# Cross-attention: the context's low part and the key norms' inverse root from VectorE to GpSimd, the denominators' first refining step kept in PSUM

## The reference

```
q = rmsnorm((x @ Wq) by head) * gq          k = rmsnorm((ctx @ Wk) by head) * gk      v = (ctx @ Wv) by head
rmsnorm(u) = u * rsqrt(mean(u * u) + 1e-5)
attn = softmax(q k^T / sqrt(128))            out = (attn v, all heads side by side) @ Wo
x = layernorm(x + self_attention(x));  x = layernorm(x + cross_attention(x, ctx));  x = layernorm(x + mlp(x))
```

## Time and profile before

| what | value |
|---|---|
| time, median of 3 runs | 1498.09 us (1496.63 to 1501.16) |
| the profiled execution's own time | 1501.96 us |
| its span, first to last instruction | 1500.1 us |
| mean granted TensorE clock | 0.987 of full speed |
| busy: TensorE | 1381.0 us, 92% |
| busy: VectorE | 1408.0 us, 94% |
| busy: ScalarE | 913.0 us, 61% |
| busy: GpSimd | 976.8 us, 65% |

### The profile page before, as it was taken

How to read it: one execution, slowest core, us unless ns; L and a number is a source line. 1 busy time by engine, 2 the same in 40 slices (tenths; PEclk the granted TensorE clock), 3 DMA queues, 4 the chain that set the end, 5 groups by cost and what they waited for, 6 DMA issues and landing times. The chain is left out here.

```text
span 1500.1 us, 23822 instructions
## 1 busy us (share of the span) xinstructions
PE 1381.0 (92%) x6430; PEld 1009.6 (67%) x6430; DVE 1408.0 (94%) x2023; ACT 913.0 (61%) x2744; POOL 976.8 (65%) x770
## 2 busy tenths in 40 slices
PE   7799899999999999999999999999999999988888
PEld 4678677666666666666666666666666666655678
DVE  5889799999999999999999999999999999999785
ACT  2645576666666666666666666666666666643443
POOL 4600005788777777887778777878787778876340
PEclk9899999999999999999999999999999999999999
DMA  6040010010101010101010101010101000010200
GB/s 224 30 150 1 23 42 21 1 41 1 42 1 42 1 42 0 41 1 41 1 41 1 39 3 34 8 32 10 32 11 31 11 15 6 20 59 1 86 1 25
DMA packets 17927, 45.56 MB, mean 30 GB/s; under 512 B 1600, under 2 KB 11968, under 8 KB 17040
## 3 DMA queue, kind: packets, MB, share of 16 engines
q1 hardware_dynamic: 17088, 44.24, 9.0%
q10 hardware_dynamic: 720, 0.10, 0.0%
HBM read 40.41 MB, written 3.93 MB: 30 GB/s over the span
## 5 line engine op out<-in xcount | busy, mean ns | idle before, releaser
L941 POOL TENSOR_TENSOR xa_scores<-xa_scores,xa_gmax 125x448 f32<-125x448 f32 x352 | 469.6, 1338 | 187.2 <-ACT xa_gmax L987 170.7
L1134 PE MATMUL xa_k_ps<-wk_parts,xa_ctxT_hi 128*125 128x512 f32 x768 | 428.6, 558 | 6.2 <-DVE wk_parts L1127 4.7
L888 POOL TENSOR_TENSOR xa_den<-probs,xa_den 125x448 f32<-125x448 f32 x311 | 370.4, 1191 | 86.4 <-ACT probs L1001 74.6
L980 ACT ACTIVATE xa_k_ps<-xa_k_ps 125x128 f32<-125x128 f32 x720 | 190.1, 264 | 324.6 <-DVE xa_ss L1060 220.7
L1071 DVE TENSOR_TENSOR xa_cmax<-xa_scores,xa_cmax 125x448 f32<-125x448 f32 x320 | 359.1, 1122 | 0.7
L1201 PE MATMUL xa_o_ps<-probs,xa_ctx_nat 125*128 125x448 f32 x768 | 352.7, 540 | 0.0
L1060 DVE TENSOR_REDUCE xa_ss<-xa_sq 125x6 f32<-125x768 f32 x360 | 337.2, 937 | 0.0
L1135 PE MATMUL xa_k_ps<-wk_parts,xa_ctxT_hi 128*125 128x512 f32 x768 | 303.8, 396 | 0.0
L1136 PE MATMUL xa_k_ps<-wk_parts,xa_ctxT_lo 128*125 128x512 f32 x768 | 303.8, 396 | 0.0
L982 ACT ACTIVATE xa_sq<-xa_k_ps 125x768 f32<-125x768 f32 x360 | 287.8, 799 | 0.0
L1001 ACT ACTIVATE probs<-xa_scores 125x448 f32<-125x448 f32 x384 | 219.3, 572 | 42.4 <-DVE xa_scores L1097 40.1
(11 more groups left out here) (170 smaller groups left out, 1754.4 us busy)
## 6 DMA issues: line engine op xcount, KB each, us to landing
ctxT_in<-in_ctxT SPq DMA_DIRECT2D x16, 750.0 KB, 9.1
xa_ctx_nat<-in_ctx SPq DMA_DIRECT2D x16, 750.0 KB
qo<-in_xq_w SPq DMA_DIRECT2D x1, 2048.0 KB, 11.1
qo<-in_xo_w SPq DMA_DIRECT2D x1, 2048.0 KB, 19.0
vo_scratch<-qo SPq DMA_DIRECT2D x2, 1024.0 KB, 4.2
vo<-vo_scratch SPq DMA_DIRECT2D x1, 2048.0 KB, 8.1
xq_wkT<-in_xk_wT SPq DMA_DIRECT2D x4, 256.0 KB, 4.2
probs<-in_xk_w SPq DMA_DIRECT2D x1, 1024.0 KB, 8.6
```

Of the source, the lines that this page charges most:

```text
L888: eng.tensor_tensor(den[:, hy, :], probs[0:KP, y % NPR, :], den[:, hy, :], ALU.add).then_inc(den_done, 1)
L941: pool.tensor_tensor(score_slot(y), score_slot(y), gmax[:, (y // KT) % 2, :], ALU.subtract).then_inc(shift_done, 1)
L980: act.activation(own, own, ACT.Square, accum_out=ss[:, j // 2, head:head + 1])
L1134: pe.matmul(out, l_hi, r_hi, start=True, stop=False)
```

## The change

Three things move. (1) `split_low`, the low part of the context, goes from VectorE to GpSimd; there it stands at the *start* of every fourth step, ahead of the subtraction, where on VectorE it stood at the end. (2) The Newton step on the key norms' inverse root goes to GpSimd as `refine_rk`, ahead of the subtraction of steps 2 and 14. GpSimd gets it in four operations on two tensors, for which a column of the constant 1.5 / sqrt(128) (`c15`) is broadcast, and the factors are folded into others: VectorE's mean is halved and scaled by `HALF`, which ScalarE's ln takes out again. (3) The closing's first result is written back to its bank of PSUM instead of to `cmax`, so the bank comes free (`s_taken`) after the second instruction instead of after the first.

```diff
--- before.py
+++ after.py
@@ -717,6 +717,7 @@
 EARLY = 3
 WH = 6
 QC = 4
+HALF = 0.5 * XD ** -0.5
 QW = UW // QC
 MAX_TURN, MAX_SPREAD = 1, 2
 
@@ -832,6 +833,7 @@
         nt = lg
         rk = sb("xa_rk", [KP, 2, KT, XH])
         ones = sb("xa_ones", [KP, 1])
+        c15 = sb("xa_c15", [KP, 1])
         ident = sb("xa_ident", [P, P], F32R)
         ident_in = probs[:, NPR - 1, 0:P]
         qmax = sb("xa_qmax", [QW, QC], F32R)
@@ -919,19 +921,47 @@
         @block.gpsimd
         def _(pool):
             pool.memset(ones[:, :], 1.0).then_inc(ones_set, 1)
-            pool.wait_ge(ones_set, 1)
+            pool.memset(c15[:, :], 1.5 * XD ** -0.5).then_inc(ones_set, 1)
+            pool.wait_ge(ones_set, 2)
 
             def q_low(ph, h):
                 pool.wait_ge(qhi_ready, ph.at(2, h + 1))
                 pool.tensor_tensor(q_lo[:, h, :, :], qo[:, UH * h:UH * h + UH, ph.tokens()],
                                    q_hi[:, h, :, :].bitcast(F32), ALU.subtract).then_inc(qlo_ready, 1)
 
+            def split_low(ph, c):
+                i = ph.parity()
+                pool.wait_ge(hi_ready, ph.at(KT // 2, c + 1))
+                pool.tensor_tensor(ctxT_lo[:, i, 2 * c:2 * c + 2, :], ctxT_in[:, i, 2 * c:2 * c + 2, :],
+                                   ctxT_hi[:, i, 2 * c:2 * c + 2, :].bitcast(F32), ALU.subtract).then_inc(lo_ready, 1)
+
+            def refine_rk(ph, ahead, g):
+
+                n = 3 if ahead else 2
+                rk_g = rk[:, ph.shift(ahead).parity(), g, :]
+                pool.wait_ge(table_ready, ph.at(2, n))
+                pool.tensor_tensor(nt[:, :, :], rk_g, rk_g, ALU.mult).then_inc(newton, 1)
+                pool.wait_ge(newton, ph.at(6, 3 * (n - 1) + 1))
+                pool.tensor_tensor(nt[:, :, :], nt[:, :, :], ss[:, g, :], ALU.mult).then_inc(newton, 1)
+                pool.wait_ge(newton, ph.at(6, 3 * (n - 1) + 2))
+                pool.tensor_tensor(nt[:, :, :], c15[:, :].unsqueeze(2).broadcast_to([KP, KT // 2, XH]), nt[:, :, :],
+                                   ALU.subtract).then_inc(newton, 1)
+                pool.wait_ge(newton, ph.at(6, 3 * (n - 1) + 3))
+                pool.tensor_tensor(rk_g, rk_g, nt[:, :, :], ALU.mult).then_inc(rk_ready, 1)
+
+            split_low(Phase(0), 0)
+
             def body(ph):
                 if ph.b == -1:
                     q_low(Phase(0), 0)
-                    return
                 for j in range(STEPS):
                     h, t = divmod(j, KT)
+                    if split_at(ph, j):
+                        ahead, c = split_at(ph, j)
+                        split_low(ph.shift(ahead), c)
+                    for step, ahead, g in ((13, 1, slice(0, 6)), (1, 0, slice(6, 12))):
+                        if j == step + 1 and ph.shift(ahead).within(0, 15):
+                            refine_rk(ph, ahead, g)
                     y = lagged(ph, j, SHIFT_LAG)
                     if y is not None and not vector_shifts(ph, y):
                         if y % KT == 0:
@@ -1004,7 +1034,7 @@
                         if j == step and ph.shift(ahead).within(0, 15):
                             n = ph.at(2, 3 if ahead else 2)
                             act.wait_ge(mean_ready, n)
-                            act.activation(lg[:, :, :], ss[:, g, :], ACT.Ln).then_inc(ln_ready, 1)
+                            act.activation(lg[:, :, :], ss[:, g, :], ACT.Ln, scale=1.0 / HALF).then_inc(ln_ready, 1)
                             act.wait_ge(ln_ready, n)
                             act.activation(rk[:, ph.shift(ahead).parity(), g, :], lg[:, :, :], ACT.Exp, scale=-0.5
                                            ).then_inc(table_ready, 1)
@@ -1028,12 +1058,6 @@
 
         @block.vector
         def _(dve):
-            def split_low(ph, c):
-                i = ph.parity()
-                dve.wait_ge(hi_ready, ph.at(KT // 2, c + 1))
-                dve.tensor_tensor(ctxT_lo[:, i, 2 * c:2 * c + 2, :], ctxT_in[:, i, 2 * c:2 * c + 2, :],
-                                  ctxT_hi[:, i, 2 * c:2 * c + 2, :].bitcast(F32), ALU.subtract).then_inc(lo_ready, 1)
-
             def body(ph):
                 for j in range(STEPS):
                     h, t = divmod(j, KT)
@@ -1076,19 +1100,8 @@
                         n = 3 if ahead else 2
                         if j == step:
                             dve.wait_ge(summed, ph.at(STEPS, STEPS + KT if ahead else STEPS))
-                            dve.tensor_scalar(ss[:, g, :], ss[:, g, :], 1.0 / XD, RMS_EPS, ALU.mult, ALU.add
+                            dve.tensor_scalar(ss[:, g, :], ss[:, g, :], HALF / XD, HALF * RMS_EPS, ALU.mult, ALU.add
                                               ).then_inc(mean_ready, 1)
-                        if j == step + 1:
-                            dve.wait_ge(table_ready, ph.at(2, n))
-                            count = [0]
-
-                            def link(ins):
-                                count[0] += 1
-                                ins.then_inc(newton, 1)
-                                dve.wait_ge(newton, ph.at(6, 3 * (n - 1) + count[0]))
-
-                            rsqrt_refine(dve, link, rk[:, ph.shift(ahead).parity(), g, :], ss[:, g, :], nt[:, :, :],
-                                         XD ** -0.5).then_inc(rk_ready, 1)
                     y = lagged(ph, j, SHIFT_LAG)
                     if y is not None and vector_shifts(ph, y):
                         if y % KT == 0:
@@ -1101,26 +1114,20 @@
                         add_den(dve, ph, y)
                     if closes(ph, j):
 
-
-                        rd = cmax[:, 1 - h, :]
+                        rd = s_ps[:, bank_d(ph, h), 0:UW]
                         dve.wait_ge(den_table, ph.at(2, h - 1))
-                        dve.tensor_tensor(rd, s_ps[:, bank_d(ph, h), 0:UW], rden[:, :], ALU.mult
-                                          ).then_inc(s_taken, 1)
+                        dve.tensor_tensor(rd, rd, rden[:, :], ALU.mult).then_inc(den_step, 1)
+                        dve.wait_ge(den_step, ph.at(2, h - 1))
+                        dve.scalar_tensor_tensor(rden[:, :], rd, 2.0, rden[:, :], ALU.subtract, ALU.mult
+                                                 ).then_inc(s_taken, 1)
                         dve.wait_ge(s_taken, pos_d(ph, h) + 1)
-                        dve.scalar_tensor_tensor(rden[:, :], rd, 2.0, rden[:, :], ALU.subtract, ALU.mult
-                                                 ).then_inc(den_step, 1)
-                        dve.wait_ge(den_step, ph.at(2, h - 1))
                         dve.wait_ge(pv_done, ph.at(STEPS, KT * (h - 1)))
                         dve.scalar_tensor_tensor(qo[:, UH * h:UH * h + UH, ph.shift(-1).tokens()],
                                                  o_ps[:, h, 0:UW].rearrange("p (g q) -> p g q", q=T), -1.0,
                                                  rden[:, :].rearrange("p (g q) -> p g q", q=T), ALU.mult, ALU.mult
                                                  ).then_inc(o_taken, 1)
-                    if split_at(ph, j):
-                        ahead, c = split_at(ph, j)
-                        split_low(ph.shift(ahead), c)
 
             dve.wait_ge(wk_loaded, 16)
-            split_low(Phase(0), 0)
             for c in range(4):
                 part = slice(c * 512, (c + 1) * 512)
                 dve.wait_ge(wk_hi_ready, c + 1)
@@ -1207,7 +1214,7 @@
                         pe.matmul(early_ps[:, n, 0:E], qo[:, head, n * P:(n + 1) * P], vo[:, head, :],
                                   start=(head == 0), stop=(head == XH - 1))
 
-            pe.wait_ge(ones_set, 1)
+            pe.wait_ge(ones_set, 2)
             pe.wait_ge(ident_ready, 1)
             each_phase(pe, body, 14)
```

## The result

The changed kernel takes 1408.97 us (median of 4 runs, 1408.63 to 1411.96), the one before in the same comparison 1498.59: a ratio of 0.9405, 95% interval 0.9386 to 0.9425. It is faster by 5.95%, 90 us. The forecast was 1436, with a range of 1405 to 1482.

What follows compares the result with a forecast made beforehand. VectorE, 98.6% busy, was taken to bound the steady halves; 37.95 to 36.0 us a half gives 54.6, plus 5, 2 and 0.4 outside, 62 off 1501.96: 1440, or 1436 allowing for the median; range 1405 to 1482.

Steps and rivals of the forecast that it cites:

- Prices: Forecast operation times: a split on GpSimd 0.75 us, the root's four operations there 1.6, the closing's second step on VectorE 0.61.
- Each of the three terms: Forecast engine times a half in the steady part: VectorE 32 us, GpSimd 34.1, TensorE 34.5.
- three so close never fit perfectly: I give 1.5 us to it: Steady part: 1.5 us a half added to the largest engine time for in-order queues waiting on each other, giving 36.0.
- rival C: Steady part: GpSimd's work hides fully and TensorE binds at 34.9 us a half, 1405 us; chance 0.15.
- A: The forecast itself: 36.0 us a half in the steady part, 1436 us, own range 1420 to 1455; chance 0.52.
- Outside: Gains outside the 28 steady halves: 5 us in the first context, 0.4 from its first low half, 2 after 1326.00 us.
- its own count of 0.07 us an instruction: VectorE spans overlap the next by some 0.07 us, so each is counted less 0.07; the inverse root takes 2.7 us off.
- Rival B: The port shared by VectorE and GpSimd sets the pace, stands returning before combines: about 37.3 us a half, 1477 us; chance 0.17.
- D: Stalls merely change name: VectorE's 6.75 us a half return as lock and waits, 0 to 5 us gained, 1495; chance 0.07.
- E: Slower: the inverse root on GpSimd costs 1.2 us an operation, delaying subtraction, exponential and TensorE: 38.6 a half, 1516; chance 0.09.
- What would show it: Signs forecast for the profile after: engine busy shares, times of combine, splits and small operations, and which waits shrink or go.
- the wait before the denominators: TensorE's wait for a score bank from VectorE before the denominators' matmul, 1.6 us each, was forecast to go.

Runs made afterwards that it cites:

- root_only: The kernel before with only the inverse root's Newton step moved to GpSimd, plus a wait on ScalarE: 1451.95 us, ratio 0.9682.
- split_root: The changed kernel with the closing's first result in SBUF again: 1417.66 us, ratio 0.9462 against the kernel before.
- queries_dve: The changed kernel with the low part of the queries on VectorE at step 8 instead of GpSimd at step 6: 1417.14 us.
- queries_two: The changed kernel with the queries' low part on VectorE and the third matmul of every score left out; a test, no candidate: 1415.78 us.
- root_late: The changed kernel with the inverse root behind the subtraction and sum of steps 2 and 14 on GpSimd instead of ahead: 1417.40 us.
- one_input: The changed kernel with the ten running-maximum combines of a half replaced by reductions over one score tile; a test, no candidate: 1396.76 us.

## Why the prediction was right, and where it was off

- What bounded the kernel: right. VectorE was the longest engine, and each part alone, which takes work off it, made the kernel faster.
- Prices: the split 0.77 us for 0.75; the root 1.80 for 1.6; the closing 0.625 for 0.61. GpSimd 967.07 / 28 = 34.5 us a half for 34.1; VectorE 887.11 / 28 = 31.7 for 32; TensorE 34.74 for 34.5. Each of the three terms is within 0.4 us. VectorE's came out by other terms than forecast: the combine was to stay at 1150 to 1300 ns and fell to 1076, while the first combine (0.5 us more) and the mean (0.9 more), which the sum didn't have, stand instead. That these cancel is luck.
- The step that failed is "three so close never fit perfectly: I give 1.5 us to it". The half came out at 34.75, TensorE's own time: the loss is none. 36.0 - 34.75 = 1.25 us, over the 27 halves of the steady part 34 us, covers the whole miss. What came is rival C's time (34.9 a half, 1405), which had a chance of 0.15, though C had TensorE alone binding and GpSimd is as full; the time is outside A's own range of 1420 to 1455, and inside the whole range by 4 us, because that took in half of C.
- A loss of such a kind does occur: `root_only` is 1.8 us above 34.75, `split_root`, `queries_dve`, `queries_two` and `root_late` are 0.2 to 0.4 above it, `queries_two` although TensorE has only 32.35 us to do there. VectorE's busy share alone does not tell where: it is 92 to 94% in the first four, but 91% in `root_late` as in the changed kernel. What decides was not found.
- Outside: 5.4 us were forecast ahead and 2 behind. By the closings 8.2 lie ahead and 0.7 behind, and the 27 halves between gave 84.4 where 27 x 1.95 = 52.7 were forecast; this last difference, 31.7 us, is the error, for the whole profiled execution came out at 1408.63 where 1440 was forecast.
- A slip in the working: by its own count of 0.07 us an instruction, the four of the inverse root are 2.85 - 0.28 = 2.57 us, and the sum took off 0.15. It is 0.1 us a half and changes nothing.
- Rival B: VectorE's stands did come back in new places (1091, 1103), but the combines stood less, so the sum stayed at 31.7. D is excluded by the time. E asked for 1.2 us an operation; it is 0.45, and in the half shown 0.7 us of lateness passes no further than ScalarE.
- What would show it: VectorE's share 89% forecast, 91% measured; GpSimd 95, measured 99; its wait for the maximum under 2 us a half, measured 0; the wait before the denominators is gone; the splits 0.77 us within 0.65 to 0.85; of the four small ones, 0.3 to 0.5 forecast, one is at 0.66. Missed: the combine, forecast at 1150 to 1300 ns, is at 1076. ScalarE waits 36 us for subtractions in 800, 1.6 a half, not the long wait of B or E. "TensorE nearly without waits, towards C" is what came.

## What to carry to other kernels

Work out each engine's time for one round of the steady loop, in starts and not in busy shares, and take the largest. Whether to add something for coupling is not settled here: in the changed kernel it was nothing, in its neighbours 0.2 to 0.4 us of 34.75 and in `root_only` 1.8. Where two engines are at the same height, a run that relieves one of them shows only that the other is there: relieve both, and each alone. Work moved off a full engine does not all stay gone (3.5 us left VectorE with the split, 2.5 came off the half), since other instructions stand in its place. And the last stretch of a pipeline, with other work on its engines, can have another bound: look at it by itself.

## What was not expected of the hardware

- A VectorE operation with one SBUF input can stand too: the mean, a multiply and add with constants on 125 x 96 values from SBUF to SBUF, takes 0.20 us while GpSimd rests and 1.12 beside it, while the reduction of the squares (line 1084), of one SBUF input also, keeps 936 to 943 ns in every run, and the one of `one_input` 608. The Trainium skill (SBUF - State Buffer, Who interferes with whom) has such a multiply-add among those that can take the shared pair and a reduction among those that never do; the rows agree.
- The turns are not symmetric: a combine of 0.61 us lengthens GpSimd's subtraction from about 1.15 to 1.53 us only, by 0.38 to 0.40, as if part of GpSimd's time did not need the port (not tested).
- TensorE is shown as 100% busy where GpSimd binds just as well. The busy share doesn't tell the two apart; the pair of runs did.
